# Expert blocks of a four-layer kernel: thirteen early and closed blocks in a written-out order, in place of nine

## The chip, the cores and the metric

One Trainium2 chip, one of its NeuronCores. The metric is the device time of one execution in microseconds (us), the median of several runs. Engine names as in the profile: PE is TensorE (PEld its weight loads), DVE is VectorE, ACT is ScalarE, POOL is GpSimd, SP is SyncE.

## The reference

`x` is 16 samples of 128 rows of 128 numbers, and goes through four layers, each chosen or scaled by a per-sample id:

```python
# L0: one of 8 feed-forward networks per sample, residual, layer norm with the expert's gain and shift
h = gelu(x @ Wi[e] + bi[e]);  x = layernorm(h @ Wo[e] + bo[e] + x) * gamma[e] + beta[e]
# L1: norm, film factors from a small hypernetwork, a router, two of 8 experts for every row
h = film(layernorm(x));  probs = softmax(h @ router_w);  gates, idx = top_k(probs, 2)
y = sum over the row's two experts of gates * (relu(h @ exp_w1[e] + b1[e]) @ exp_w2[e] + b2[e]);  x = x + y
# L2: a rotation of neighbouring columns by two angles per sample
# L3: a narrow adapter (128 to 32 to 32 to 128) with one of 16 expert matrices per sample, residual, layer norm
x = layernorm(up(expert_W[d] @ gelu(down(x))) + x) * gamma + beta
```

All of it is float32.

## The kernel before

**Halves and blocks.** The 16 samples are worked in four groups of four, and the expert layer in two halves of eight samples (groups 0 and 1, groups 2 and 3). Each row of 128 numbers goes to two experts, so a half has 2048 row copies. They are sorted by expert into blocks of 128 row copies, one expert per block. The full blocks of the first half can be worked before the second half has been routed: at least 9 exist, and these 9 are the early blocks (`EARLY`). What the first half leaves over is filled up with rows of the second half: together at most 39 blocks (`NBLK`), 9 early and 30 late.

**One block** passes through five engines. POOL gathers its 128 rows from `h_rows` in memory with an indirect DMA (`gather`, L536). PE transposes them (`rows_T`, L975), ACT copies the transpose out of PSUM (`transposed`, L716). PE multiplies by the block's expert matrix of 512 columns (`blk_up`, L808), which SP has loaded (`load_w1`, L440), ACT adds the bias and applies relu in four pieces (`hidden`, L726), PE multiplies back to 128 columns (`blk_down`, L808). DVE adds the expert's second bias and writes `y_blk` (`add_b2`, L1475), and POOL scatters the 128 rows to `token_rows` in memory (`scatter`, L542).

**What sets the order.** There is no scheduler: each engine runs its own program, a loop over step `k`, and semaphores hold the engines together. In step `k` PE does `blk_up(k)`, `blk_down(k-2)` and the transpose of block `k+3`; ACT does `hidden(k)` and then `transposed(k+3)`; DVE adds the bias of block `k-1`. Into the steps of the early blocks the routing of the second half is put: `z_transposes` (L877), `row_stats`, `film_h` (L631), `route`, `top2` (L1269 to L1280), `rank`, the sorting of rows into slots (`sort_slots`, `hot_blocks`, `hot_slots` L1374, `hot_tiles`, `hot_rows` L694) and `inverse`, a product on PE that turns slots into row numbers. It ends in `sources` (L1416 to L1421), which writes the row numbers `src_i` of the late blocks. `store_rows` (L639) writes the second half's `h_rows`.

**POOL's order.** The gathers of early blocks, with small powers between them for the norms (L522), then four scatters (`HELD`), then, once the late row numbers are there, four gathers, and from there one scatter and one gather in turn, the gather nine blocks ahead (`LEAD`).

**The end.** From step 30 on (`BEGIN3`) the adapter layer L3 runs for the first half in four units of two samples, two steps per unit, beside the last late blocks: `combine` on DVE (L1484, L1492) joins the two gated expert rows that SP has loaded back (`load_y`), PE does `l3_T`, `l3_down`, `l3_residual`, `l3_up`, DVE takes the statistics (`stats3`) and the inverse root by three Newton steps (`root3`). When the last block has been scattered, SP loads the second half's rows and units 4 to 7 follow.

## Time and profile before

| what | us |
|---|---|
| median of 3 runs (lowest, highest) | 231.68 (230.59, 233.28) |
| the profiled execution, its own time | 230.44 |
| its span, first to last instruction | 228.6 |
| time around the span | 1.84 |
| PE busy, share of the span | 178.3, 78% |
| DVE, ACT, POOL busy | 116.6, 107.2, 109.0 |
| mean granted TensorE clock | 0.842 of 2.4 GHz |

Times in the rows further down count from the span's start. Where a row ends in square brackets, it gives the time for which the engine sat idle just before, and after the arrow what ended it; "issue" means nothing that the profile shows. PE and PEld rows of a matrix product count two instructions for one float32 product. The granted clock is given as a share of full speed, so that 0.50 stands for 1.2 GHz and 1.00 for 2.4 GHz.

### The profile page before, as it was taken

The numbers are of one execution on the slowest core, as the hardware profiler recorded it, in microseconds if no ns is written. First come the engines' busy times: TensorE is split into PE (matmuls) and PEld (weight loads), VectorE is DVE, ScalarE is ACT, GpSimd is POOL, SyncE is SP. The second block draws the span as 40 slices with busy tenths as digits, with TensorE's granted clock in tenths as the row PEclk, the third lists the DMA queues.
The fourth block names the chain that finished last, engine by engine and source line by source line (L and its number), as shares of the span: only waits on it lengthen the run. The fifth ranks groups of instructions, "written<-read, shape, count | busy, mean of one in ns | idle before, by whom it ended". The sixth has DMA issues, their size and how long they took to land.

```text
span 228.6 us, 5312 instructions
## 1 busy us (share of the span) xinstructions
PE 178.3 (78%) x1287; PEld 161.6 (71%) x1287; DVE 116.6 (51%) x575; ACT 107.2 (47%) x338; POOL 109.0 (48%) x126
## 2 busy tenths in 40 slices
PE   6999997999959599284799888887799994077920
PEld 6999986898859599173798777876688873045710
DVE  6316798888943868940023343311236777353460
ACT  3564874665235566301566556564356651123310
POOL 5126335102870670127777777777776333101560
PEclk9999999997667859857589999999999999555555
DMA  6999999994643113047456565535951011330001
GB/s 205 294 322 337 329 317 301 250 292 123 220 130 100 26 34 106 1 104 231 137 154 186 156 173 146 147 97 173 319 167 57 26 46 47 106 134 1 26 25 44
DMA packets 35048, 34.82 MB, mean 152 GB/s; under 512 B 3793, under 2 KB 26475, under 8 KB 35019
## 3 DMA queue, kind: packets, MB, share of 16 engines
q1 hardware_dynamic: 27995, 26.56, 40.3%
q0 software_dynamic: 2496, 5.12, 7.5%
q10 hardware_dynamic: 4528, 2.81, 4.0%
q8 instruction: 12, 0.20, 0.4%
q14 instruction: 17, 0.14, 0.2%
HBM read 29.81 MB, written 4.65 MB: 151 GB/s over the span
## 4 chain that ended last, share of the span: by engine, by line
PE 35%; DVE 21%; POOL 19%; issue 11%; DMA 9%; DVEq 2%; ACT 1%; ACTq 0%; POOLq 0%; SPq 0%
PE bank L808 31%; POOL got L536 7%; POOL token_rows L542 7%; DMA got<-h_rows,src_i 6%; DVE st L1196 3%; PE bank L975 1%; POOL rstd L522 1%; DVE hot_in L1374 1%; POOL rs L556 1%; DVEq L1598 1%; DMA token_rows<-y_blk,dst_i 1%; DMA w_place<-token_rows 1%; DVE y_blk L1475 1%; DVE top_i L1272 1%; PE bank L1004 1%
## 5 line engine op out<-in xcount | busy, mean ns | idle before, releaser
L726 ACT ACTIVATE hid<-bank,small 128x128 f32<-128x128 f32 x156 | 44.4, 368 | 28.0 <-PE bank L808 27.2
L808 PE MATMUL bank<-w,hid 128*128 x312 | 46.5, 297 | 5.3 <-DVE y_blk L1475 4.8
L542 POOL DMA_INDIRECT token_rows<-y_blk,dst_i x39 | 38.8, 995 | 23.0 <-DVE y_blk L1475 13.4
L536 POOL DMA_INDIRECT got<-h_rows,src_i x39 | 38.2, 981 | 22.2 <-issue 10.1
L808 PE MATMUL bank<-gotT,w_now 128*128 128x128 f32 x312 | 46.8, 299 | 0.0
L808 PEld LDWEIGHTS bank<-w,hid 128*128 128x128 f32 x312 | 42.1, 209 | 6.3 <-issue 6.0
L808 PEld LDWEIGHTS bank<-gotT,w_now 128*128 128x128 f32 x312 | 42.9, 213 | 0.0
L1475 DVE TENSOR_TENSOR y_blk<-bank,b_tab 128x128 f32<-128x128 f32 x39 | 11.4, 291 | 58.5 <-PE bank L808 57.0
L975 PE MATMUL bank<-ident,got 128*128 128x128 f32 x39 | 13.0, 334 | 18.0 <-DMA got<-h_rows,src_i 13.2
L716 ACT ACTIVATE gotT<-bank 128x128 f32<-128x128 f32 x39 | 11.0, 282 | 27.2 <-PE bank L975 26.9
L667 ACT ACTIVATE act<-bank,small 128x128 f32<-128x128 f32 x64 | 18.0, 374 | 11.9 <-PE bank L808 11.5
L522 POOL TENSOR_TENSOR rstd<-veps,minus_half 128x4 f32<-128x4 f32 x12 | 12.3, 1027 | 20.9 <-DVE veps L1244 9.1
L975 PEld LDWEIGHTS bank<-ident,got 128*128 128x128 f32 x39 | 6.2, 160 | 22.4 <-DMA got<-h_rows,src_i 16.9
L808 PE MATMUL bank<-w_place,act 128*128 128x128 f32 x128 | 17.5, 279 | 0.7 <-ACT act L667 0.7
L808 PE MATMUL bank<-xT,w_place 128*128 128x128 f32 x128 | 17.1, 276 | 0.0
L808 PEld LDWEIGHTS bank<-w_place,act 128*128 128x128 f32 x128 | 15.5, 192 | 1.0 <-ACT act L667 0.9
L808 PEld LDWEIGHTS bank<-xT,w_place 128*128 128x128 f32 x128 | 15.6, 192 | 0.1
L1004 PE MATMUL bank<-ident,xbT 128*128 128x128 f32 x16 | 4.5, 372 | 10.7 <-DVE xbT L1492 10.7
L556 POOL TENSOR_TENSOR rs<-ve,minus_half 128x2 f32<-128x2 f32 x4 | 2.9, 714 | 18.6 <-DVE ve L1505 18.6
L1004 PEld LDWEIGHTS bank<-ident,xbT 128*128 128x128 f32 x16 | 2.3, 167 | 11.9 <-DVE xbT L1492 11.2
L749 ACT ACTIVATE zg<-bank,nmr,rs 128x128 f32<-128x128 f32 x14 | 5.6, 453 | 9.8 <-DVE nmr L1530 9.8
L808 PE MATMUL bank<-ident 128*128 128x128 f32 x38 | 8.4, 399 | 1.9 <-POOL minus_half L496 1.9
(232 smaller groups left out, 267.8 us busy)
## 6 DMA issues: line engine op xcount, KB each, us to landing
w_now<-in_exp_w SPq DMA_DIRECT2D x39, 256.0 KB, 3.3
w_place<-in_l_wi SPq DMA_DIRECT2D x16, 256.0 KB, 5.2
w_place<-in_l_wo SPq DMA_DIRECT2D x16, 256.0 KB, 5.6
rows<-in_l_rows SPq DMA_DIRECT2D x16, 128.0 KB, 4.9
w<-in_exp_w SPq DMA_DIRECT2D x8, 256.0 KB, 5.8
w_place<-token_rows SPq DMA_DIRECT2D x8, 256.0 KB, 3.5
x_sb<-in_x ACTq DMA_DIRECT2D x4, 256.0 KB, 4.5
h_rows<-h_row ACTq DMA_DIRECT2D x4, 256.0 KB, 2.8
```

The costliest lines, as they stand in the source:

```text
L522: g_.tensor_tensor(rstd[:, kind, g % 2, :], veps[:, kind, g % 2, :], minus_half[:], ALU.pow)\
L536: g_.indirect_dma_start(got[:, n % RING, :], None, h_dram[0:(HB if n < EARLY else NB) * P], bass.IndirectOffsetOnAxis(ap=src_i[:, n:n + 1] ...
L542: g_.indirect_dma_start(y_dram, bass.IndirectOffsetOnAxis(ap=dst_i[:, n:n + 1], axis=0), y_blk[:, n % YRING, :], None).then_inc(st_y[n % Y ...
L667: last = a_.activation(act0[:, b % 2, c, :], up_bank(b)[:, c * P:(c + 1) * P], ACT.Gelu, bias=cols[:, bass.ds(e * FC + (R_BI + c), 1)])
L716: a_.activation(gotT[:, n % TRING, :], got_bank, ACT.Copy).then_inc(a_gT, 1)
L726: last = a_.activation(hid[:, n % HRING, c, :], up_bank(n)[:, c * P:(c + 1) * P], ACT.Relu, bias=cols[:, bass.ds(e * FC + (R_B1 + c), 1)])
L749: last = a_.activation(z3[:, i, :], o3_bank[u][:, k * P:(k + 1) * P], ACT.Identity, bias=nmr3[:, i:i + 1], scale=rs3[:, i:i + 1])
L808: return t_.matmul(out_, lhsT, rhs, start=start, stop=stop)
L975: t_.transpose(got_bank, got[:, n % RING, :], ident[:]).then_inc(p_gT, 1)
L1004: last = t_.transpose(uT_bank[u][:, k * P:(k + 1) * P], u_b[:, place(u) + k, :], ident[:])
L1196: do(v_.bn_stats(st[:, kind, g % 2, k, :], src(k)))
L1475: v_.tensor_tensor(y_blk[:, n % YRING, :], y_bank(n), b2_tab[:, bass.ds(e, 1), :].rearrange("p o d -> p (o d)"), ALU.add)\
```

## The change

**More early blocks.** Besides the 9 blocks that are sure to be full, up to 4 blocks of the first half that are not full are closed: no row of the second half is put into them. So 13 blocks are early. Closing costs blocks: at most 41 are needed in place of 39, 13 early and 28 late.

**Order written out.** On PE and ACT the early blocks are no longer in the loop; their order stands as a list. PE does the transpose of block `k` right before `blk_up(k)`, not three blocks ahead, and ACT does `transposed(k)`, `hidden(k)` and then the copy of block `k-2`. The eight warming products ahead of the first block are gone, the two expert preparations `experts3(2)` and `experts3(3)` stand behind the last early block, and `inverse(2)` behind the transpose of block 12.

**The second bias.** For early blocks ACT copies the product out of PSUM (`evac_y`) and POOL adds the bias just before it scatters; for late blocks DVE goes on adding it. ACT also does the norm of groups 2 and 3 (`norm1`), which was DVE's. DVE's program has the whole routing of the second half in one piece.

**The end.** L3 of the first half begins at step 36 of 41 in place of 30 of 39, so that its last unit and most of its norms run behind the last block. Their inverse roots and shifts go to POOL, but for the first unit. PE reads L3's expert numbers ahead (`l3_which`).

**Small things.** `hot_slots` is two wide comparisons in place of sixteen narrow ones. `store_rows` stands earlier. The second half's last unit but one is normalised on DVE in place of ACT and POOL.

```diff
-    NBLK = (TOPK * NB * S + E1 * (P - 1)) // P
-    EARLY = -((E1 * (P - 1) - TOPK * HB * S) // P)
+    SURE = -((E1 * (P - 1) - TOPK * HB * S) // P)
+    CLOSED = 4
+    EARLY = SURE + CLOSED
...
-    RING, YRING, TRING, WRING, HRING = 16, 12, 4, 6, 3
+    RING, YRING, TRING, WRING, HRING = 16, 10, 4, 6, 3
     LEAD = 9
-    HELD = 4
+    HELD = 5
+    FIRST_OUT = 4
-    BEGIN3 = 30
+    BEGIN3 = 36
...
             def scatter(n):
-                pool.wait_ge(v_y, n + 1)
+                if n < EARLY:
+                    pool.wait_ge(a_y, n + 1)
+                    e = pool.value_load(exp_i[0:1, n:n + 1], min_val=0, max_val=E1 - 1)
+                    ch.do(g_.tensor_tensor(y_blk[:, n % YRING, :], y_blk[:, n % YRING, :],
+                                           b2_tab[:, bass.ds(e, 1), :].rearrange("p o d -> p (o d)"), ALU.add))
+                    ch.settle()
+                else:
+                    pool.wait_ge(v_y, n - EARLY + 1)
...
+                if n >= 9:
+                    scatter(n - 9)
-            hot_tiles(1)
-            for n in range(HELD):
-                scatter(n)
             hot_tiles(2)
+            for n in range(FIRST_OUT, HELD):
+                scatter(n)
...
+            for k in range(EARLY):
+                transposed(k)
+                if k == 2:
+                    norm1(2)
+                if k == 3:
+                    norm1(3)
+                if k == 5:
+                    film_h(2)
+                    film_h(3)
+                hidden(k, block_expert(k))
+                if k >= BEHIND:
+                    evac_y(k - BEHIND)
+                if k == 6:
+                    store_rows(2)
+                if k == 7:
+                    store_rows(3)
+                    hot_rows(1)
+                if k == 11:
+                    hot_rows(2)
...
-            keep_warm(8, bank[6], ident[:])
...
+            rows_T(7)
+            rank(1)
+            rows_back(2)
+            blk_up(7)
+            down_of(5)
+            rows_T(8)
+            rows_back(3)
+            blk_up(8)
+            down_of(6)
...
+            rows_T(12)
+            inverse(2)
+            blk_up(12)
+            down_of(10)
+            down_of(11)
+            down_of(12)
+            experts3(2)
+            experts3(3)
+            pe.wait_ge(v_exp, 2)
...
-                for j in range(first, past):
-                    last = v_.tensor_scalar(hot_in[:, h, j, :], col_bf[:], in_blk[:, j:j + 1], None, ALU.is_equal)
+                v_.tensor_tensor(hot_in[:, h, first:past, :],
+                                 col_bf[:].rearrange("p (o n) -> p o n", o=1).to_broadcast([P, n, P]),
+                                 in_blk_bf[:, first:past].rearrange("p (j o) -> p j o", o=1).to_broadcast([P, n, P]),
+                                 ALU.is_equal).then_inc(v_hot, 1)
...
-                if 2 <= u < HU + 2 and odd == 0:
-                    stats3(u - 2)
-                    shift_of_norm3(u - 2)
+                if u == 2 and odd == 0:
+                    stats3(0)
+                    root3(0)
+                    shift_of_norm3(0)
```

**ACT, one early block.** `gotT` is the transposed block, `hid` the hidden rows that the relu writes, `y_blk` the block's result. Before, the copy of a transpose stands between the hidden rows of two blocks and belongs to a block three further on:

```order
L719 TENSOR_LOAD exp_i
L719 ISA x2
L716 ACTIVATE gotT<-bank 128x128
L726 ISA
L726 ACTIVATE hid<-bank,small 128x128
L726 ISA
L726 ACTIVATE hid<-bank,small 128x128
```

With the change the block's own transpose comes first, then its hidden rows, then the copy of an older result, and only then the next block's transpose:

```order
L744 ACTIVATE gotT<-bank 128x128
L747 TENSOR_LOAD exp_i
L747 ISA x2
L754 ISA
L754 ACTIVATE hid<-bank,small 128x128
L754 ISA
L754 ACTIVATE hid<-bank,small 128x128
L754 ISA
L754 ACTIVATE hid<-bank,small 128x128
L754 ISA
L754 ACTIVATE hid<-bank,small 128x128
L795 ACTIVATE y_blk<-bank 128x128
```

What moved is the transpose of the next block, from two blocks ahead of its use to right behind the hidden rows of the block before.

**PE, before the second half's last routing product.** `gotT,w_now` is `blk_up`, `ident,got` a block's transpose, `hot_blk,hot_in` the product `inverse`. Before, the first part of `inverse` for the late blocks stands right ahead of block 8's `blk_up`, whose transpose was done steps earlier:

```order
L808 MATMUL bank<-w,hid 128x128
L808 MATMUL bank<-hot_blk,hot_in 128x60 x16
L808 MATMUL bank<-gotT,w_now 128x128 x4
L1042 TENSOR_LOAD exp_i
L1042 ISA x2
L808 ISA
L808 MATMUL bank<-w,hid 128x128
```

With the change each `blk_up` has its own transpose right ahead of it, here that of block 10 with the first part of `inverse` between:

```order
L1034 MATMUL bank<-ident,got 128x128
L865 MATMUL bank<-hot_blk,hot_in 128x56 x16
L865 MATMUL bank<-gotT,w_now 128x128 x4
L1102 TENSOR_LOAD exp_i
L1102 ISA x2
L865 ISA
L865 MATMUL bank<-w,hid 128x128
```

What moved is the transpose, which now waits for a gather and is waited for within one step; the second part of `inverse` stands in the same way behind the transpose of block 12.

**POOL, where the late row numbers arrive.** `got` is a gathered block, `token_rows` the memory that results are scattered to. Before, four gathers and then one scatter and one gather in turn:

```order
L528 TENSOR_TENSOR hot_blk<-hot_tmp,col_bf 128x16x30
L536 DMA got<-h_rows,src_i 128x128 x4
L542 DMA token_rows<-y_blk,dst_i 12288x128
L536 DMA got<-h_rows,src_i 128x128
L542 DMA token_rows<-y_blk,dst_i 12288x128
L536 DMA got<-h_rows,src_i 128x128
```

With the change one gather, and then a scatter that has the addition of the bias ahead of it:

```order
L548 DMA got<-h_rows,src_i 128x128
L555 TENSOR_LOAD exp_i
L555 ISA x2
L556 ISA
L556 TENSOR_TENSOR y_blk<-y_blk,b_tab 128x128
L561 DMA token_rows<-y_blk,dst_i 12288x128
L548 DMA got<-h_rows,src_i 128x128
L555 TENSOR_LOAD exp_i
L555 ISA x2
L556 ISA
```

Eight such scatters (blocks 5 to 12) are left at that point, where five plain ones (blocks 4 to 8) were, and each has one late gather behind it.

## Rows read from the trace of the kernel before

**Rows 1.** Chain of work that ended last: start us, us, what.

```profile
86.38 0.29 DVE top_v L1269 x4
...
101.35 1.00 POOL got L536
...
102.66 3.49 DMA got<-h_rows,src_i
```

**Rows 2.** Timeline, from the early row numbers to the sorting: start us, us, engine, instruction.

```profile
54.57 0.17 DVE L1421 TENSOR_SCALAR src_i<-dst_i 128x9 int32<-128x9 int32 x1
...
84.83 0.39 DVE L1269 MAX8 top_v<-bank 128x8 f32<-128x8 f32 x4 [0.37 <-issue]
...
88.63 0.60 ACT L639 ACTIVATE h_row<-bank 128x512 f32<-128x512 f32 x1 [0.38 <-PE bank L894]
...
89.25 0.37 ACTq L641 DMA_DIRECT2D h_rows<-h_row  x1
...
90.21 0.62 PE L808 MATMUL bank<-hot_blk,hot_in 128*128 128x60 bf16 x16
...
93.58 3.48 DVE L1374 TENSOR_SCALAR hot_in<-col_bf,in_blk 128x128 bf16<-128x128 bf16 x16
```

**Rows 3.** Timeline, one step of a block at full and at half clock.

```profile
61.43 0.28 ACT L716 ACTIVATE gotT<-bank 128x128 f32<-128x128 f32 x1 [2.82 <-PE bank L975]
...
61.82 0.14 PEld L975 LDWEIGHTS bank<-ident,got 128*128 128x128 f32 x1 [0.73 <-issue]
...
111.95 1.83 PEld L808 LDWEIGHTS bank<-gotT,w_now 128*128 128x128 f32 x8
...
114.23 1.14 ACT L726 ACTIVATE hid<-bank,small 128x128 f32<-128x128 f32 x4 [0.61 <-PE bank L808]
...
119.40 0.97 PEld L808 LDWEIGHTS bank<-gotT,w_now 128*128 128x128 f32 x8
...
120.72 1.14 ACT L726 ACTIVATE hid<-bank,small 128x128 f32<-128x128 f32 x4 [0.37 <-PE bank L808]
...
121.73 0.29 ACT L716 ACTIVATE gotT<-bank 128x128 f32<-128x128 f32 x1
```

**Rows 4.** Windows: stretch, length, busy us (x instructions) of PE, PEld, DVE, ACT, POOL, clock, DMA, GB/s.

```profile
54.00:58.00 4.00, 4.00 (x24) 3.06 (x21) 3.73 (x21) 1.31 (x3) 2.04 (x2) 0.52 0.46 135
...
72.00:78.00 6.00, 4.07 (x37) 3.87 (x35) 4.85 (x30) 1.82 (x7) 3.35 (x4) 1.00 0.05 12
78.00:82.00 4.00, 3.64 (x17) 3.64 (x18) 3.42 (x12) 4.00 (x14) 2.76 (x3) 0.51 0.07 18
...
135.00:150.00 15.00, 12.42 (x97) 11.03 (x96) 5.22 (x11) 9.63 (x32) 11.64 (x12) 1.00 0.54 146
...
191.00:200.00 9.00, 0.07 (x1) 0.00 (x0) 4.63 (x22) 0.81 (x2) 1.84 (x2) 0.67 0.32 97
200.00:210.00 10.00, 7.80 (x28) 5.26 (x28) 5.29 (x22) 2.52 (x7) 0.75 (x1) 0.50 0.22 78
```

**Rows 5.** Groups by line, shapes apart: busy us, mean ns of one, idle before.

```profile
L631 ACT ACTIVATE hT<-bank,film 128x128 f32<-128x128 f32 x16 | 6.1, 495 | 6.4 <-DVE film L1262 6.4
...
L548 POOL TENSOR_TENSOR zg<-zg,rows 128x256 f32<-128x256 f32 x3 | 2.2, 726 | 0.0
...
L694 ACT ACTIVATE hot_blk<-hot_tmp,pair_no 128x240 bf16<-128x240 bf16 x4 | 1.8, 529 | 0.6 <-DVE hot_tmp L1367 0.6
...
L1367 DVE TENSOR_TENSOR hot_tmp<-col_bf,blk_of_bf 128x480 bf16<-128x480 bf16 x2 | 1.3, 657 | 0.4 <-issue 0.4
```

**Rows 6.** Timeline, the last gather and transpose, the last addition, the second half's first unit.

```profile
172.53 0.97 POOL L536 DMA_INDIRECT got<-h_rows,src_i  x1 [0.30 <-PE bank L975]
...
178.21 0.27 PE L975 MATMUL bank<-ident,got 128*128 128x128 f32 x1
...
194.51 0.29 DVE L1475 TENSOR_TENSOR y_blk<-bank,b_tab 128x128 f32<-128x128 f32 x1
...
200.51 0.61 DVE L1484 SCALAR_TENSOR_TENSOR z<-w_place,gates,x 128x128 f32<-128x128 f32 x2 [4.13 <-DMA w_place<-token_rows]
```

More of the change, by code:

```diff
@@ L46, in conditional_layers_kernel, with most_blocks @@
     KT = TOPK * HB
-    NBLK = (TOPK * NB * S + E1 * (P - 1)) // P
-    EARLY = -((E1 * (P - 1) - TOPK * HB * S) // P)
+    SURE = -((E1 * (P - 1) - TOPK * HB * S) // P)
+    CLOSED = 4
+    EARLY = SURE + CLOSED
+    def most_blocks(full):
+        closed = max(EARLY - full, 0)
+        held = min((E1 - closed) * (P - 1), TOPK * HB * S - full * P)
+        return full + closed + (TOPK * HB * S + held + E1 * (P - 1)) // P
+    NBLK = max(most_blocks(full) for full in range(SURE, TOPK * HB * S // P + 1))
     LATE = NBLK - EARLY
@@ L474, in _ @@
                         load_y(u)
-            for u in range(HU):
-                store_out(u)
+            store_out(0)
             scattered(NBLK)
@@ L479, in _ @@
                 load_y(u)
-            for u in range(HU, NU):
+            for u in range(1, NU):
                 store_out(u)
@@ L687, in _ @@
                     film_h(1)
-                if b == 14:
-                    store_rows(0)
+                if b >= 13 and b < 13 + HG:
+                    store_rows(b - 13)
             def hot_rows(s):
@@ L705, in _ @@
             a_.activation(warm[:, 2, :], ones_row[:], ACT.Exp).then_inc(ac, 1)
-            for i in range(NG):
-                evac_m3(i)
+            evac_m3(0)
+            evac_m3(1)
             for i in range(E3, MT):
@@ L744, in norm3 @@
                 act.wait_ge(v_nmr3, u + 1)
-                if earlier(u) is not None:
-                    act.wait_ge(v_o3, earlier(u) + 1)
+                if earlier(u) == 0:
+                    act.wait_ge(v_o3, 1)
+                elif earlier(u) is not None:
+                    act.wait_ge(g_o3, earlier(u))
                 for k in unit(u):
@@ L1590, in _ @@
             l0_spread_shift(3)
+            minus_mean(2)
             l1_stats(3)
-            l1_norm(2)
-            l1_norm(3)
+            hot_blocks(1)
+            minus_mean(3)
+            later_bases()
+            row_stats(2)
+            row_stats(3)
+            film_factors(2)
+            film_factors(3)
+            part_experts()
+            top2(2)
+            top2(3)
+            ranks(1)
+            more_blocks()
+            sort_slots(1)
+            hot_blocks(2)
+            hot_slots(1, 0, KT // 2)
@@ L1652, in _ @@
+            combine(HU - 1, unit(HU - 1))
+            scale_shift3(0)
+            stats3(1)
+            stats3(2)
+            shift_of_norm3(1)
+            shift_of_norm3(2)
             combine(HU, unit(HU))
+            stats3(3)
             combine(HU + 1, unit(HU + 1))
+            shift_of_norm3(3)
             combine(HU + 2, unit(HU + 2))
```

321 lines of the change are left out of this document (178 added, 143 removed).

## The prediction

> **What bounds the kernel now.** I read the chain of waits first. It shows three stages behind the first layer. Until 101.35 the chain goes through DVE's ranking and sorting of the second half, top values from 86.38 on [rows 1]. Then POOL issues the first late gather, and the next 1.31 us later (102.66 [rows 1]); from there one issue follows another. The last of the 30 late gathers is issued at 172.53 [rows 6]. Between the two lie 29 gathers and 26 scatters, 55 issues in 71.2 us, 1.294 us each: a block costs POOL 2.59 us, and POOL paces this stage. PE is busy 12.42 of 15 us in it at full clock [rows 4]. Third comes the end. The last transpose runs at 178.21, the last addition of the bias at 194.51, and the second half's first unit starts 6.0 us later, when its rows are back [rows 6]. From the last addition to the end of the execution there are 230.44 - 194.51 = 35.9 us.
>
> So the time is a sum of three: when the late row numbers arrive, how long POOL needs to the last gather, and how long it takes from there to the last addition. I go through the change by these.
>
> **Part 1: the early blocks, up to the late row numbers.** Block 0 can be gathered once its row numbers exist, at 54.74 before [rows 2]. The change widens the comparisons: DVE took 3.48 us for sixteen when the second half was sorted [rows 2]; the nearest row for a wide one is 657 ns for 480 elements [rows 5], in proportion 1.40 us for 1024, 2.8 us for two. Against that stand four small instructions more for the closed blocks, 0.17 us each by the row of `src_i` [rows 2]. I take no difference, with 1 us either way as bound. Gather 0 is issued at about 55.1 and lands 3.5 us later, as the first late one did, 3.49 [rows 1]: 58.6. PE stood at half clock from 54 on, 0.52 [rows 4], and the warming products are gone, so the first steps run at half.
>
> The Trainium skill, "VectorE: DVE Perf Modes", section on the perf-mode tier table, says that a two-tensor operation on 16-bit data runs at two elements per cycle. The row above, 16-bit throughout, is at 1.37 ns an element and does not show it; by the rule the row numbers would come about 1 us earlier and the total would be 1 us less.
>
> Now one step. ACT's program runs transposed copy, hidden rows, copy of an older result, next transposed copy, and PE's `blk_up` waits for the transposed copy: a ring. At full clock: from `blk_up` to the hidden rows 119.40 to 120.72, 1.32 us; to ACT's next start 121.73, 1.01; the copy of the older result about 0.26, a quarter of the four hidden pieces; from transposed copy to PE's next start 61.43 to 61.82, 0.39 [rows 3]. Together 3.0 us. At half clock the first link is 111.95 to 114.23, 2.28 [rows 3], and the ring 3.7 without and 3.94 with the older copy, 4.6 where that copy waits for PE's `blk_down`, which at half comes 1.8 us later (the weight loads of 1.83 [rows 3]).
>
> Starts of `blk_up` so: block 0 at 59.5 (landing, transpose, copy). Blocks 1 and 2 at 63.2 and 66.9, half clock. Block 3 at 71.5 (4.6), block 4 at 75.8 (4.3), by when I take the clock to have risen, since PE is then busy without a gap. Block 5 at 78.8 (3.0). In step 5 two `film_h` stand in the ring, 6.1 / 4 = 1.5 us each [rows 5], of which 1.3 is covered by `blk_up`: 1.6 more, block 6 at 83.4. In step 6 ACT's `store_rows(2)` waits for PE's `rows_back(2)`, that for `rank`, that for `top2(3)` on DVE, that for `route(3)`, which stands behind `blk_up(6)`. `blk_up` takes 0.97 [rows 3], `route` has as many products, from the start of `top2(3)` to `store_rows` it was 86.38 to 88.63, 2.25 us, and `store_rows` takes 0.60 and its DMA's issue 0.37 [rows 1, 2]; with the transposed copy that is 5.7: block 7 at 89.1. Step 7 holds `store_rows(3)`, 1.0 us, and `hot_rows(1)`, two of 0.529 that overlap a little (1.8 / 2 = 0.9 a pair [rows 5]): block 8 at 94.0. Three steps of 3.0 bring block 11 to 103.0. Behind its hidden rows ACT copies block 9 and does `hot_rows(2)`, until 106.5. Only then can PE do `inverse(2)`, 0.62, and DVE the row numbers, three instructions of 0.17 with a wait ahead of each, some 0.7 [rows 2]. DVE's own sorting is long done by then, since its program no longer waits for blocks. First late gather at 108.1 in place of 101.35: **+6.7 us**.
>
> Bounds: at full clock from the start, 4.2 us less (0.7, 0.7, 1.6, 1.2 in the first four steps); at half clock to the end, 8 steps x 1.5 = 12 us more.
>
> **Part 2: POOL to the last gather.** The late gathers are 13 to 40, and between first and last stand 27 more gathers and 27 scatters: 54 x 1.294 = 69.9 us. Closing has made two blocks more, which is why this is hardly less than the 71.2 before. Eight scatters carry an addition. No such instruction is in the trace of before; the nearest is POOL's 128x256 at 726 ns [rows 5], so 128x128 lies between 0.36 and 0.73; I take 0.55. The expert number is read ahead of it: DVE idled 0.37 us where it read one [rows 2]. POOL's queue could hide that (0) or take 0.6. I take 0.9, between 0.35 and 1.3: 8 x 0.9 = 7.2, from 2.8 to 10.4. Behind a scatter so delayed the next gather is queued, and PE waits for that one, so nothing covers it. Sum 77.1 in place of 71.2: **+5.9 us**. Last gather at 185.2.
>
> **Part 3: from the last gather to the last addition.** Before, 172.53 to 194.51, 22.0 us: PE was late (last transpose 178.21, not 176.0, where the gather landed), and PE had nothing left from 191.1 on (0.07 us busy in the window from 191 [rows 4]) while DVE did statistics and Newton steps ahead of the last addition, 3.4 us. With the change PE has only begun with L3 when the last gather lands, 3.5 us after its issue; and only unit 0's statistics stand in DVE's loop, three blocks ahead of the end. From the last transpose to PE's end it was 191.1 - 178.2 = 12.9 us; the same products and half a unit more of L3, less waiting, 13.2. So 3.5 + 13.2 = 16.7: **-5.3 us**.
>
> **Part 4: behind the last addition.** DVE now does there what it did before: `combine(3)`, `scale_shift3(0)`, statistics of units 1 and 2. It was idle 4.13 us before the second half's rows came [rows 6] and was busy 4.63 in the window from 191 [rows 4], so the work about fits. Behind it one more unit's statistics stand between two combines; the numbers read ahead and the last unit but one on DVE save about as much. I take **0**, from -3.9 (half of the 7.8 us for which PE is busy at clock 0.50 from 200 to 210 [rows 4], if its new work keeps the clock up) to +2.
>
> **Sum.** 6.7 + 5.9 - 5.3 + 0 = +7.3 on the profiled execution's own 230.44 is 237.7. That execution was 0.5% under the median of the runs shown, 231.68; I say 238. About 1% is what a measurement of this kernel can tell from no change.
>
> **The clock.** Early blocks leave PE idle about a third of each step. For a clock that holds: 12.42 of 15 us busy holds 1.00, and 72 to 78 held it with 4.07 of 6. Against: 78 to 82 is at 0.51 behind it, and 200 to 210 stays at 0.50 although PE is busy 7.80 of 10 us [rows 4]. The Trainium skill, "TensorE: Matmul & The Clock Gate", section on what is actually happening, calls the slow clock the default that activity releases. The last window shows busy time that released nothing; by the rule alone part 1 stands, by that window its upper bound does.
>
> **Rivals.**
> *No change (0.17).* The clock is full from block 0 (-4.2) and POOL reads expert numbers while it still issues (2.8 in place of 7.2, -4.4): 237.7 - 8.6 = 229.1, within 1% of 230.44. For it: 72 to 78. Against: PE is idle ahead of block 0.
> *Faster (0.16).* The ring doesn't bind: steps come at the pace of the busiest engine, 2.0 us for PE, as the late blocks come at about 1.9 when nothing is awaited (hidden rows at 120.72, `blk_up` 119.40 [rows 3]). Then the DVE sorting sets the row numbers, at some 97, 11 us sooner: 226.6. For it: neither PE nor ACT has more than 2 us of work in a step. Against: the order rows, in which the next transposed copy stands behind the hidden rows. It decides from a mean of 3.2 us per step from block 0 to 12 (mine is 3.85); below that the change gains.
> *Much slower (0.10).* PE stays at half clock through the early blocks: +12, 249.7.
> The forecast itself has 0.57.
>
> **How the numbers follow.** Faster by over 1%: 0.16, the ring rival. Within 1%: 0.17. Slower by over 1%: 0.57 + 0.10 = 0.67. The likeliest case alone runs from 233 to 243, additions and single clock drops; the range reaches to the no-change case and to about the middle of the way to the half-clock case: 228.5 to 246.
>
> **What would show it.** The first late gather between 106 and 111; hidden rows of neighbouring early blocks 3.0 us apart at full clock; POOL's additions 0.4 to 0.7 us and pairs of about 3.5 us for eight blocks; the last gather to the last addition about 17 us. Wrong if the first late gather comes by 101, if early steps stand 2 us apart, or if the eight pairs come at 2.6.

## The result and the profile after

The changed kernel takes 239.01 us (median of 4 runs, 236.76 to 239.58) against 231.13 of the kernel before on the same chip: ratio 1.040, 95% interval 1.034 to 1.046. The forecast was 238.0. The profiled execution took 238.47, its span is 236.7, the mean granted clock 0.829 in place of 0.842. By the prediction's four parts, each from the rows below and [rows 1, 6]:

| part | before | after | change | forecast |
|---|---|---|---|---|
| start to the first late gather | 101.35 | 111.41 | +10.1 | +6.7 |
| first to last late gather | 71.2 | 73.3 | +2.1 | +5.9 |
| last gather to last addition | 22.0 | 18.4 | -3.6 | -5.3 |
| last addition to the execution's end | 35.9 | 35.4 | -0.6 | 0 |
| sum | 230.44 | 238.47 | +8.0 | +7.3 |

The chain of waits of the changed kernel, part of the early stage (start us, us, what). It answers to [rows 1]:

```profile
87.61 0.92 PE bank L954 x4
88.56 0.61 ACT h_row L668
89.19 0.37 ACTq L670
89.65 0.29 ACT gotT L744
89.98 3.78 PE bank L865 x16
...
103.60 1.17 PE bank L865 x8
105.21 0.51 ACT hid L754 x2
...
106.45 2.05 PE bank L865 x16
```

Before, the chain went through DVE's sorting here. Now it alternates between PE and ACT: that is the ring. At 87.61 it shows something more, the rows' way back on PE, the storing of rows on ACT and its DMA issue, one behind the other, before the next transposed copy.

The timeline of the changed kernel, one plain step at full clock and then the starts of `blk_up` of blocks 6 to 8 (start us, us, engine, instruction, idle before). It answers to [rows 3]:

```profile
75.87 0.97 PEld L865 LDWEIGHTS bank<-gotT,w_now 128*128 128x128 f32 x8 [0.48 <-ACT gotT L744]
77.19 1.14 ACT L754 ACTIVATE hid<-bank,small 128x128 f32<-128x128 f32 x4 [1.36 <-PE bank L865]
78.20 0.29 ACT L795 ACTIVATE y_blk<-bank 128x128 f32<-128x128 f32 x1
78.36 0.30 ACT L744 ACTIVATE gotT<-bank 128x128 f32<-128x128 f32 x1
78.72 0.97 PEld L865 LDWEIGHTS bank<-gotT,w_now 128*128 128x128 f32 x8 [0.92 <-ACT gotT L744]
82.88 0.97 PEld L865 LDWEIGHTS bank<-gotT,w_now 128*128 128x128 f32 x8 [1.30 <-ACT gotT L744]
89.98 1.78 PEld L865 LDWEIGHTS bank<-gotT,w_now 128*128 128x128 f32 x8 [1.86 <-ACT gotT L744]
96.80 0.97 PEld L865 LDWEIGHTS bank<-gotT,w_now 128*128 128x128 f32 x8 [2.39 <-ACT gotT L744]
```

PE waits for ACT's transposed copy ahead of each of these. The plain step takes 2.85 us (75.87 to 78.72): 1.32 to the hidden rows, 1.01 and 0.16 to the next transposed copy, 0.36 back to PE. The two steps behind block 6 take 7.10 and 6.82.

The windows of the changed kernel (stretch, length, busy us and instructions of PE, PEld, DVE, ACT, POOL, clock, DMA share, GB/s). They answer to [rows 4]:

```profile
59.00:66.00 7.00, 4.51 (x18) 3.85 (x19) 5.22 (x28) 1.59 (x6) 5.86 (x6) 0.50 0.66 206
...
78.00:82.00 4.00, 2.99 (x26) 2.86 (x25) 3.65 (x13) 4.00 (x15) 3.31 (x5) 1.00 0.57 148
82.00:90.00 8.00, 5.66 (x32) 5.19 (x32) 5.25 (x41) 3.13 (x11) 6.50 (x9) 0.63 0.32 85
90.00:100.00 10.00, 7.86 (x38) 7.26 (x38) 7.21 (x18) 4.30 (x14) 7.11 (x7) 0.67 0.33 94
100.00:111.00 11.00, 8.38 (x90) 7.76 (x90) 0.41 (x3) 5.54 (x22) 0.00 (x0) 0.95 0.32 107
...
185.00:203.00 18.00, 16.17 (x122) 13.80 (x120) 6.77 (x31) 8.52 (x28) 8.42 (x9) 1.00 0.11 38
...
210.00:220.00 10.00, 8.37 (x31) 5.56 (x30) 6.46 (x26) 3.05 (x8) 4.21 (x6) 0.50 0.23 71
```

The clock is at half in the first steps, full from 78 to 82, and lower again from 82 to 100. From 100 to 111 POOL does nothing and DVE almost nothing: POOL waits for the late row numbers, and DVE for the product on PE from which it computes them.

POOL's timeline in the changed kernel, where these arrive:

```profile
111.41 0.97 POOL L548 DMA_INDIRECT got<-h_rows,src_i  x1 [13.39 <-DVE src_i L1544]
112.41 0.47 POOL L556 TENSOR_TENSOR y_blk<-y_blk,b_tab 128x128 f32<-128x128 f32 x1
113.15 0.98 POOL L561 DMA_INDIRECT token_rows<-y_blk,dst_i  x1 [0.28 <-ACT y_blk L795]
114.43 0.97 POOL L548 DMA_INDIRECT got<-h_rows,src_i  x1 [0.30 <-issue]
```

POOL had been idle for 13.39 us. From gather to gather, with one scatter and its addition between, it takes 3.02.

The timeline of the changed kernel at the end, which answers to [rows 6]: last gather, last transpose and last addition:

```profile
184.71 0.98 POOL L548 DMA_INDIRECT got<-h_rows,src_i  x1 [0.30 <-issue]
...
187.22 0.33 PE L1034 MATMUL bank<-ident,got 128*128 128x128 f32 x1
...
203.12 0.29 DVE L1598 TENSOR_TENSOR y_blk<-bank,b_tab 128x128 f32<-128x128 f32 x1 [3.21 <-PE bank L865]
```

The last addition waits for PE, which is busy 16.17 of the 18 us before it. The chain of waits of the changed kernel shows for what PE itself waited there (start us, us, what):

```profile
195.57 0.41 DVE st L1623 x2
...
198.79 0.81 ACT zg L779 x2
199.65 0.71 PE bank L865 x4
200.37 1.45 issue
201.82 1.17 PE bank L865 x8
```

The groups by line, shapes apart, give the sizes of two new instructions (busy us, mean ns of one, idle before), beside [rows 5]:

```profile
L556 POOL TENSOR_TENSOR y_blk<-y_blk,b_tab 128x128 f32<-128x128 f32 x13 | 7.0, 540 | 0.3
...
L1489 DVE TENSOR_TENSOR hot_in<-col_bf,in_blk_bf 128x1024 bf16<-128x1024 bf16 x4 | 5.8, 1487 | 0.0
```

### The profile page after: what moved, and what is told of

The parts are those of the page before. It is cut to its first block, busy times and chain, and to the rows that moved or that the text cites. A ratio compares the mean times of both kernels' runs of the same rounds, so it can differ in the third digit from the quotient of the medians.

```text
span 236.7 us, 5387 instructions
## 1 busy us (share of the span) xinstructions
PE 186.8 (79%) x1305; PEld 167.0 (71%) x1305; DVE 107.2 (45%) x499; ACT 114.5 (48%) x367; POOL 127.0 (54%) x150
## 4 chain that ended last, share of the span: by engine, by line
PE 36%; POOL 14%; DMA 13%; issue 13%; DVE 11%; ACT 5%; ACTq 2%; POOLq 1%; DVEq 0%
PE bank L865 32%; DMA got<-h_rows,src_i 9%; POOL got L548 6%; POOL token_rows L561 5%; DMA small<-in_small 2%; ACT hid L754 2%; PE bank L1034 2%; DMA w_place<-token_rows 1%; DVE hot_in L1489 1%; DVE st L1303 1%; DVE xbT L1615 1%; ACT gotT L744 1%; DMA token_rows<-y_blk,dst_i 1%; POOL y_blk L556 1%; ACT hT L660 1%
## 5 line engine op out<-in xcount | busy, mean ns | idle before, releaser
L754 ACT ACTIVATE hid<-bank,small 128x128 f32<-128x128 f32 x164 | 46.9, 370 | 42.0 <-PE bank L865 42.0
L865 PE MATMUL bank<-gotT,w_now 128*128 128x128 f32 x328 | 53.4, 315 | 10.1 <-ACT gotT L744 8.8
L865 PEld LDWEIGHTS bank<-gotT,w_now 128*128 128x128 f32 x328 | 47.9, 224 | 13.2 <-ACT gotT L744 11.5
L865 PE MATMUL bank<-w,hid 128*128 x328 | 50.1, 301 | 1.7 <-issue 1.6
L865 PEld LDWEIGHTS bank<-w,hid 128*128 128x128 f32 x328 | 45.1, 213 | 3.0 <-issue 2.6
L1598 DVE TENSOR_TENSOR y_blk<-bank,b_tab 128x128 f32<-128x128 f32 x28 | 8.2, 292 | 64.3 <-PE bank L865 62.8
L1034 PE MATMUL bank<-ident,got 128*128 128x128 f32 x41 | 14.0, 341 | 18.4 <-DMA got<-h_rows,src_i 17.6
L534 POOL TENSOR_TENSOR rstd<-veps,minus_half 128x4 f32<-128x4 f32 x12 | 12.7, 1058 | 22.1 <-DVE veps L1354 10.1
L1303 DVE BATCH_NORM_STATS2 st<-bank 128x6 f32<-128x128 f32 x32 | 7.1, 283 | 9.5 <-PE bank L937 6.3
L865 PE MATMUL bank<-x_sb,xT 128*128 128x128 f32 x32 | 8.2, 401 | 1.6 <-ACT zg L779 1.6
L865 PEld LDWEIGHTS bank<-x_sb,xT 128*128 128x128 f32 x32 | 6.2, 273 | 4.2 <-ACT zg L779 2.3
L528 POOL TENSOR_TENSOR xbT<-xT,bo_cols 128x512 f32<-128x512 f32 x4 | 4.3, 1066 | 8.8 <-ACT xT L652 4.6
```

Of the source, the lines that this page charges most:

```text
L528: g_.tensor_tensor(xbT[:, g % 2].rearrange("p (b s) -> p b s", b=GS), xT[:, g % 2].rearrange("p (b s) -> p b s", b=GS), over_tokens(bo_col ...
L534: g_.tensor_tensor(rstd[:, kind, g % 2, :], veps[:, kind, g % 2, :], minus_half[:], ALU.pow)\
L754: last = a_.activation(hid[:, n % HRING, c, :], up_bank(n)[:, c * P:(c + 1) * P], ACT.Relu, bias=cols[:, bass.ds(e * FC + (R_B1 + c), 1)])
L865: return t_.matmul(out_, lhsT, rhs, start=start, stop=stop)
L1034: t_.transpose(got_bank, got[:, n % RING, :], ident[:]).then_inc(p_gT, 1)
L1303: do(v_.bn_stats(st[:, kind, g % 2, k, :], src(k)))
```

## The experiments

The theory after reading the two traces: the late row numbers come 10 us later because the product that gives them stands at the end of thirteen early steps, and these are long because each block's transpose, its copy, its products and its hidden rows stand one behind the other on PE and ACT. The rivals: the clock; the routing of the second half; POOL's additions; the two blocks more; or that PE would be no sooner whatever comes earlier. Each kernel starts from the changed one, 239.01 us. The kernel before ran beside each group of them and took 229.4 to 231.0 us there, where it took 231.13 beside the changed one; so of a difference to 239.01 up to 1.8 us can lie in this, and the ratio to the kernel before (1.040 for the changed one) is given as well. Block 0 is transposed between 58.8 and 61.7 in the executions read, so first late gathers of two kernels compare to some 2 us; steps from block to block compare better.

**The ring undone.** PE transposes block k+1 ahead of the products of block k, ACT copies it ahead of the hidden rows of block k.

```diff
+            transposed(0)
             for k in range(EARLY):
-                transposed(k)
+                if k + 1 < EARLY:
+                    transposed(k + 1)
...
             rows_T(0)
-            blk_up(0)
             rows_T(1)
+            blk_up(0)
+            rows_T(2)
             blk_up(1)
...
```

> The changed kernel with one thing undone in the written-out order: PE transposes block k+1 ahead of the products of block k, and ACT copies that transpose ahead of the hidden rows of block k. Theory (the early blocks are slow because transposed copy, products, hidden rows and next transposed copy form a ring of 2.85 us per step): neighbouring hidden rows come 2.0 to 2.5 us apart where nothing else is awaited, PE idles less so that its clock falls less, the first late gather comes at 101 to 106 in place of 111.4, and the total is 5 to 10 us below the changed kernel, 229 to 234. Rival (the early stage is set by the clock and by what the routing of the second half waits for, not by the ring): steps stay at 2.8 us or more, first late gather 110 or later, total within 2 us of 239.

Measured: 226.4 us, 12.6 less, more than the theory asked; 0.980 of the kernel before (0.971 to 0.989). The timeline of this kernel, six starts of `blk_up` (blocks 0 to 2 and 9 to 11) and the first late gather:

```profile
62.79 1.91 PE L867 MATMUL bank<-gotT,w_now 128*128 128x128 f32 x8
...
65.25 1.91 PE L867 MATMUL bank<-gotT,w_now 128*128 128x128 f32 x8
...
67.17 1.86 PE L867 MATMUL bank<-gotT,w_now 128*128 128x128 f32 x8
...
90.88 1.12 PE L867 MATMUL bank<-gotT,w_now 128*128 128x128 f32 x8
...
93.35 1.14 PE L867 MATMUL bank<-gotT,w_now 128*128 128x128 f32 x8
...
95.33 1.06 PE L867 MATMUL bank<-gotT,w_now 128*128 128x128 f32 x8
...
100.19 0.97 POOL L548 DMA_INDIRECT got<-h_rows,src_i  x1 [4.33 <-DVE src_i L1546]
```

Blocks 9 to 11, at full clock, give steps of 2.47 (a part of the product for the row numbers is in it) and 1.98, where a plain step of the changed kernel takes 2.85; at half clock, which both kernels have in their first steps (0.50 from 60 to 66 in the changed one, from 62 to 68 in this), 2.46 and 1.92 in place of 3.59. So the ring shows at either level of the clock. The first late gather comes at 100.19. Hidden rows of blocks 0 and 12 stand 35.5 us apart (64.86 to 100.39), 2.96 a step, where the changed kernel's `blk_up` needs 4.14 (60.63 to 110.29). The ring is the main cost, and without it the rest of the change is a gain. The 12.6 us are not the plain steps alone. `blk_up` of blocks 0 and 12 stands 36.3 us apart here (62.79 to 99.09) in place of 49.7, 13.4 less; 6.5 of these lie in the two steps behind block 6 (7.5 in place of 13.9), in which the routing no longer stands in a ring and the clock is higher (0.79 from 82 to 90 and 1.00 from 90 to 100, where the changed kernel has 0.63 and 0.67).

**The late row numbers' product two steps sooner.**

```diff
-                if k == 11:
+                if k == 8:
                     hot_rows(2)
...
             inverse(1)
+            inverse(2)
             blk_up(10)
...
-            inverse(2)
             blk_up(12)
```

> The changed kernel with the last part of the product that gives the late row numbers right behind its first part, two steps sooner (at block 10 in place of block 12), and the rows it needs from ACT at step 8 in place of 11. DVE's own sorting was done at 97.6 and waited 12.9 us. Theory (the late row numbers come late only because this product stands at the end of the early steps): first late gather at 104.5 to 106.5 in place of 111.4, total 4 to 6 us lower, 233 to 235. Rival (the early blocks themselves must be finished anyway, PE or POOL catches up no sooner): the gather comes sooner but the last addition moves by less than 2 us, total 237 or more.

Measured: first late gather at 103.45, total 233.03, 6.0 less; 1.011 of the kernel before (1.001 to 1.020). The rival falls: what comes sooner there ends sooner. The gather came 8.0 us sooner, a little more than expected; the clock was higher here too, 0.92 in place of 0.63 from 82 to 90.

**Nine scatters ahead of the first late gather** (`HELD` = 9 in place of 5).

> The changed kernel with nine scatters in place of five ahead of the first late gather (blocks 5 to 8 too), in the 13.4 us in which POOL waits for the late row numbers. Theory (POOL paces the late stage, 1.29 us an issue and 0.46 us an addition): between the first and the last late gather stand 4 scatters and 4 additions fewer, 4 x 1.75 = 7.0 us; the first late gather stays at 111.4, the last comes at 177 to 179 in place of 184.7, total 4 to 7 us lower, 232 to 235. Rival (PE is nearly as late, it is busy 21.6 of the 25 us from 160 to 185): POOL's gain turns into waits for PE, total within 2 us of 239.

Measured: 230.65 us, 8.4 less and more than expected, 1.003 of the kernel before (0.998 to 1.007). From first to last late gather it takes 66.5 us (113.89 to 180.35) in place of 73.3, so 6.8 of the 7.0 expected. The execution read took 235.54 us, well above the median, and all its gathers come late; but the kernel further down with nine scatters first and the transposes ahead needs 66.3 for the same stretch. POOL does pace the late stage, and the 13.39 us for which it stood idle were worth filling.

**The additions left out.** POOL scatters the early blocks without their second bias.

```diff
                 if n < EARLY:
                     pool.wait_ge(a_y, n + 1)
-                    e = pool.value_load(exp_i[0:1, n:n + 1], min_val=0, max_val=E1 - 1)
-                    ch.do(g_.tensor_tensor(y_blk[:, n % YRING, :], y_blk[:, n % YRING, :],
...
-                    ch.settle()
```

> The changed kernel without POOL's addition of the second bias for the early blocks (their second bias is left out of the result) and without the reading of the expert number ahead of it. Theory (an addition costs POOL 0.46 us and eight of them stand between late gathers): pairs of scatter and gather take 2.56 us from the first one, last gather 3.5 to 4 us sooner, total 3 to 4 us lower, 235 to 236. Rival (the additions are hidden, by PE or by the queue): less than 1 us.

Measured: 234.25 us, 4.8 less, 1.015 of the kernel before (1.007 to 1.022). First late gather at 111.57, last at 181.28, 69.7 us between, 3.6 less; 54 issues at 1.294 are 69.9. The rest of the 4.8 lies within the spread of both kernels' runs (236.8 to 239.6, 233.3 to 235.3).

**PE kept busy in its waits.** Products without use in the bank that the block's own products fill next.

```diff
+            def warm_up(n, count):
+                if n >= 2:
+                    pe.wait_ge(a_hid, n - 1)
+                keep_warm(count, up_bank(n), ident[:])
+
+            warm_up(0, 8)
...
             rows_T(0)
+            warm_up(0, 2)
             blk_up(0)
...
             rows_T(7)
+            warm_up(7, 6)
             rank(1)
...
```

> The changed kernel with PE kept busy in its waits of the early stage: eight products without use ahead of block 0 and two (six in steps 7 and 8) between each block's transpose and its own products. The ring of 2.85 us per step at full clock stays. If the clock's falls (0.50 from 59 to 72, and again behind 85) are a large part of what the early stage takes, the granted clock stays near 1.00 from 60 to 111, plain steps stay at 2.85 to 3.3 us, the first late gather comes at 102 to 106 in place of 111.4 and the total is 4 to 8 us lower, 231 to 235. If the clock falls all the same or the products without use stand in the ring's way, first late gather at 109 or later and total 237 or more.

Measured: 237.66 us, 1.4 less; first late gather at 110.18. This is the second case of the expectation. The gain itself isn't clear of noise: 1.030 of the kernel before (1.023 to 1.036), against 1.040 (1.034 to 1.046). The windows of this kernel:

```profile
66.00:72.00 6.00, 5.00 (x43) 4.67 (x42) 2.07 (x11) 5.14 (x18) 2.36 (x2) 1.00 0.60 185
...
82.00:90.00 8.00, 6.54 (x46) 6.29 (x45) 4.43 (x31) 2.30 (x7) 6.22 (x8) 0.79 0.38 102
90.00:100.00 10.00, 7.84 (x54) 7.42 (x53) 6.56 (x14) 4.58 (x15) 6.42 (x6) 0.83 0.31 88
```

The clock is full from 66 to 82, and blocks 0 to 6 take 19.1 us (62.05 to 81.18) in place of 22.25 (60.63 to 82.88). But the two steps behind block 6 stay at 8.0 and 6.4 us. The products ahead of the ranking and of the rows' way back take 1.9 and 1.5 us of them; without these it would be some 11.0 for both, against 13.9 in the changed kernel. So the clock is worth 3.1 us in the first steps (22.25 - 19.13) and, as an estimate, 2.9 in these two, but is not all that makes them long. The estimate takes the useless products to lie wholly in the ring, and the clock was not full in these windows (0.79 and 0.83). One of the two steps can be read without it: with the late row numbers' product two steps sooner, the order up to there the same and the clock full until 88, the step behind block 6 took 6.01 us (82.57 to 88.58) in place of 7.10, so that 1.1 us of that step were the clock's.

**No block closed**: 9 early and 30 late, the written-out order cut after block 8.

```diff
-    CLOSED = 4
+    CLOSED = 0
...
-    FIRST_OUT = 4
+    FIRST_OUT = 0
...
-    BEGIN3 = 36
+    BEGIN3 = 34
...
-                if k == 11:
+                if k == 8:
                     hot_rows(2)
...
             rows_back(3)
+            inverse(1)
             blk_up(8)
             down_of(6)
-            rows_T(9)
-            blk_up(9)
+            inverse(2)
             down_of(7)
...
             down_of(8)
...
```

> The changed kernel with no block closed: 9 early and 30 late blocks, 39 in all, its written-out order cut after block 8 (transposes still right ahead of their own block), both parts of the product for the late row numbers beside block 8, four scatters more behind the early gathers, L3 begun five steps before the end as in the changed kernel. If the closed blocks cost time because four more steps of the ring stand ahead of the late row numbers, first late gather at 98 to 101, 54 issues and 4 additions to the last gather (54 x 1.294 + 4 x 0.46 = 71.7), 18.4 and 35.3 behind it as in the changed kernel, total 223 to 227. If the written-out order costs the time whatever the number of early blocks, total 235 or more.

Measured: 230.09 us, 0.995 of the kernel before (0.990 to 1.000): between the two. First late gather at 104.58, behind both the row numbers at 102.5 and a fifth scatter at 103.30; 71.3 us to the last, as expected (71.7). The row numbers are later than I expected because blocks 7 and 8 go at half clock here too and ACT's rows for the product come at 100.45. So with the ring kept, four steps and two blocks fewer take 8.9 us off: 6.8 up to the first late gather and 2.0 from there to the last. With the ring undone thirteen blocks (226.4) beat nine with it; nine without it were not run, so what closing is worth by itself stays open.

**The routing moved aside, the ring kept.** PE does the products of blocks 7 and 8 first; ACT stores rows while it would wait for products.

```diff
             rows_T(7)
+            blk_up(7)
             rank(1)
             rows_back(2)
-            blk_up(7)
...
+            blk_up(8)
             rows_back(3)
-            blk_up(8)
...
+                if k == 8:
+                    store_rows(2)
+                if k == 9:
+                    store_rows(3)
+                    hot_rows(1)
                 hidden(k, block_expert(k))
...
-                if k == 6:
-                    store_rows(2)
-                if k == 7:
-                    store_rows(3)
-                    hot_rows(1)
```

> The changed kernel with the ring kept (each transpose right ahead of its own block) but the second half's routing moved out of it: PE does the products of blocks 7 and 8 ahead of the ranking and of the rows' way back, and ACT stores rows and prepares the one-hot rows of the second sorting stage while it would wait for the products of blocks 8 and 9 anyway, not ahead of the next transposed copy. In the changed kernel these two steps took 7.1 and 6.8 us (starts 82.88, 89.98, 96.80). If they were long because routing stood in the ring, they come to 3 to 4.5 us each, the first late gather at 104 to 107 in place of 111.4 and the total 4 to 7 us lower, 232 to 235. If they were long because the clock stood at half or because DVE was late, steps 6 to 8 stay above 6 us and the total within 2 us of 239.

Measured: 232.41 us, 6.6 less, 1.007 of the kernel before (1.004 to 1.011); first late gather at 103.64. The timeline and the windows of this kernel:

```profile
82.95 0.97 PEld L865 LDWEIGHTS bank<-gotT,w_now 128*128 128x128 f32 x8 [1.22 <-ACT gotT L744]
86.44 0.97 PEld L865 LDWEIGHTS bank<-gotT,w_now 128*128 128x128 f32 x8 [0.66 <-ACT gotT L744]
89.55 0.97 PEld L865 LDWEIGHTS bank<-gotT,w_now 128*128 128x128 f32 x8 [0.66 <-ACT gotT L744]
```

```profile
78.00:90.00 12.00, 9.39 (x79) 8.64 (x78) 9.17 (x52) 8.57 (x31) 9.80 (x13) 1.00 0.35 106
```

The steps behind block 6 take 3.49 and 3.11 us in place of 7.10 and 6.82. But the clock stays full too, and its fall in the changed kernel lies at 84, where the order of the two is still the same. So a half of the edit was run as well, ACT's part alone.

```diff
+                if k == 8:
+                    store_rows(2)
+                if k == 9:
+                    store_rows(3)
+                    hot_rows(1)
                 hidden(k, block_expert(k))
...
-                if k == 6:
-                    store_rows(2)
-                if k == 7:
-                    store_rows(3)
-                    hot_rows(1)
```

> Half of the edit that moved the routing aside: ACT stores rows and prepares the one-hot rows in the waits of steps 8 and 9, but PE still does the ranking and the rows' way back ahead of the products of blocks 7 and 8. The whole edit gave 232.41 us, steps of 3.5 and 3.1 us behind block 6, and a clock that did not fall at 85, although the order is the same as in the changed kernel up to there. If the fall of the clock at 85 belongs to the order up to block 7, it is here too (0.6 to 0.8 from 82 to 90), the two steps take 4.5 to 6 us each and the total is 234 to 237. If it doesn't fall here either, the steps take 3.5 to 5 us and the total is 232.5 to 235; then the changed kernel's fall hangs on more than the order.

Measured: 233.0 us, 6.0 less; first late gather at 105.67. Beside it the kernel before took 229.4, so the ratio, 1.019 (1.010 to 1.028), says less: about 4.7 us under the changed kernel's 1.040. Its windows:

```profile
82.00:90.00 8.00, 6.00 (x53) 5.67 (x53) 6.14 (x42) 3.93 (x17) 6.61 (x9) 1.00 0.40 110
90.00:100.00 10.00, 7.55 (x74) 6.76 (x72) 7.98 (x19) 6.43 (x25) 7.62 (x8) 1.00 0.29 85
```

The clock doesn't fall here either, and the two steps take 4.29 and 3.71 us (83.84, 88.13, 91.84). Read beside each other, both at full clock: PE's part of the edit is worth 1.4 us in these steps (8.0 against 6.6). ACT's is some 3 (11.0, the estimate above, against 8.0) and the clock's some 2.9 of the changed kernel's 13.9; these two hang on that estimate. What decides the fall stays open: of seven kernels read for this, with the same order on PE and ACT up to there, it came at 83 to 86 in four (the changed one, the one without additions, the one with nine early blocks, the one with nine scatters first), at 88 in the one with the row numbers sooner, and not at all in these two.

**Together.** First the ring undone and nine scatters first:

> The transposes one block ahead on PE and ACT (which alone gave 226.4 us) together with nine scatters ahead of the first late gather (which alone gave 230.65). If POOL still paces the late stage, the gains add: 6 to 8 us under 226.4, 218.5 to 220.5, with the first late gather at 100 and the last at 166 to 168. If PE has become the bound of the late stage (in the first of the two it was busy 19.7 of the 20 us from 160 to 180), the gain is less than 2 us, 225 or more. I expect something between, 221 to 224, because PE was idle 12 of the 49 us from 111 to 160 and earlier gathers fill that.

Measured: 222.06 us, 0.959 (0.953 to 0.965) of the kernel before; between the two, as expected. The timeline of POOL in it, around the first late gather:

```profile
101.65 0.98 POOL L561 DMA_INDIRECT token_rows<-y_blk,dst_i  x1 [0.28 <-POOL y_blk L556]
102.94 0.97 POOL L548 DMA_INDIRECT got<-h_rows,src_i  x1 [0.30 <-issue]
```

The gather no longer waits for row numbers, computed from 98.45 on, but for the scatters ahead of it. That is why the next kernel, with `inverse(2)` ahead of block 11 and `hot_rows(2)` at step 9 besides, gained nothing:

> As the run before it in this group, and the last part of the product for the late row numbers one step sooner (ahead of block 11's products in place of block 12's, ACT's rows for it after step 9 in place of 11). DVE's sorting was done at 94.9 with the transposes ahead, and its next instruction waited 4.4 us. If the row numbers still set the start of the late stage, first late gather at 97 to 99 and 1 to 3 us less than the run without this; if PE bounds the late stage, no difference.

Measured: 222.47 us, 0.964 of the kernel before (0.958 to 0.970). I had named PE as the reason for no difference; it was POOL, whose first late gather came at 100.57, 0.30 behind a scatter, although the computing of the row numbers began at 92.85. That it lies 2.4 us ahead of the 102.94 above is not the edit's doing: block 0 was transposed 2.6 us sooner in this execution (58.81 against 61.36). Then the second bias of blocks 9 to 12 by DVE (a constant `BY_ACT` = 9 in place of `EARLY` where ACT copies and POOL adds):

> Transposes ahead and nine scatters first (222.06 us), and the second bias of early blocks 9 to 12 added by DVE as for late blocks, in place of ACT's copy and POOL's addition. Four additions of 0.47 us leave POOL's path between first and last late gather: if POOL paces, 1.5 to 2 us less, 220 to 220.6; if PE does, no difference.

Measured: 221.53 us, 0.962 of the kernel before (0.955 to 0.968); 0.5 less is within the runs' spread (220.2 to 224.0), so the total doesn't tell. The traces do for POOL: from first to last late gather it is 64.5 us in place of 66.3, 1.8 of the 1.9 expected. Last, all of it, with `HELD` = 7:

> Everything that gained, together: transposes ahead, routing beside the steps, late row numbers' product ahead of block 11, seven scatters ahead of the first late gather, second bias of blocks 9 to 12 by DVE. Row numbers at about 94 (DVE's sorting done at 92 to 95), first late gather 95 to 97, then 52 issues x 1.294 + 2 x 0.47 = 68.2 to the last, 18.4 and 35.3 behind it: 217 to 220. If PE bounds the late stage whatever comes earlier, 221 or more, as with the run that had the row numbers sooner and gained nothing (222.47 against 222.06).

Measured: 220.98 us, 0.963 (0.956 to 0.971) of the kernel before. The waits of POOL from 90 to 170 in it (what waited, on what, us in total, times, longest):

```profile
POOL got L549 <- issue: 7.9, 26, 0.3
POOL token_rows L562 <- issue: 7.0, 23, 0.3
POOL token_rows L562 <- POOL y_blk L557: 1.7, 6, 0.3
POOL got L549 <- PE bank L1035: 0.6, 2, 0.3
POOL token_rows L562 <- DVE y_blk L1599: 0.6, 2, 0.3
```

POOL has no wait over 0.3 us left from 90 to the last gather. The total is 1 us above the range I gave: the row numbers were computed from 94.28 on, as expected, but POOL was not through with its seven scatters and came to the first late gather at 99.05, not at 95 to 97. From there to the last it took 67.6 (forecast 68.2) and behind it 18.4 and 35.2. The last four kernels, 220.98 to 222.47, can't be told apart; all beat both the kernel before and the changed one.

## Why the prediction was right, and where its sizes were off

**Part 1, the mechanism.** Right: the ring binds, the first late gather comes when the last early steps are done, and DVE's sorting is ready long before (its last instruction ahead of the wait at 97.42, the next at 110.52). The ring's terms were 3.0 us at full clock and 3.7 at half; measured 2.85 and 3.59 (60.63 to 64.22). Block 0 came at 60.63 (forecast 59.5), block 5 at 78.72 (78.8), block 6 at 82.88 (83.4). Undoing the ring gave back more than the whole loss.

**Part 1, the size.** The failed step is "by when I take the clock to have risen", which I then let stand for all that follows: block 7 at 89.1, block 8 at 94.0. Measured 89.98 and 96.80, 13.9 us for two steps in place of 10.6, 3.3 too little and as much as the whole miss. At full clock the same two steps come to about 11 by the estimate above, near the working's 10.6; the clock had fallen again, to 0.63 and 0.67. That block 6 was met so well (82.88 for 83.4) is partly luck: block 0 came 1.1 us late, and the six steps behind it took 22.25 us in place of 23.9. Behind block 8 the forecast ran about parallel: 9.65 us to block 11 (106.45) for 9.0, and from the start of `inverse(2)` to the first late gather 1.5 us (109.91 to 111.41), for which the working had 1.6.

**Part 2.** +2.1 in place of +5.9. The count of issues was right (54 without additions measured 69.7, working 69.9). The mis-sized term is the addition with the reading of its expert number: 0.9 taken, 0.46 measured (pairs of 3.03 against 2.56). The addition alone is 0.47 (112.41), near the 0.55 taken for it, so the reading costs POOL nothing on top; the rest of the 0.9, and the 0.6 allowed for the reading, stood on no row of POOL. The bound's lower end, 0.35, was the nearer.

**Part 3.** -3.6 in place of -5.3. The gather was transposed 2.5 us behind its issue, not 3.5, but PE then needed 15.9 us to the last addition, not 13.2. The chain shows where: unit 0's statistics and Newton steps on DVE (195.57 to 198.77) lie on it, the bit that I had put "three blocks ahead of the end", then ACT's normalising, PE's residual product, and 1.45 us in which PE waits for nothing that the profile shows ahead of the last `blk_down`. This was read, not tried.

**Part 4.** -0.6, forecast 0. PE's new work at the end didn't bring the clock up: 0.50 from 210 on, as before.

**Two rules weighed.** The wide comparisons took 1487 ns for 1024 elements, 1.45 ns each, much as the row of before had it (1.37). The Trainium skill's rate of two elements per cycle for 16-bit data ("VectorE: DVE Perf Modes", section on the perf-mode tier table) doesn't show here. One operand of these comparisons is a single number per slot, spread over 128 columns (`to_broadcast` in the diff), so they are no test of the rate for two plain tensors. With products in PE's waits the clock was at 1.00 from 66 to 72, where the changed kernel had 0.50. That agrees with the Trainium skill, "TensorE: Matmul & The Clock Gate", section on what is actually happening, by which activity releases the slow clock. The end of the kernel doesn't show it: there PE was busy 8.37 of 10 us and stayed at 0.50.

**The rivals.** "The ring doesn't bind" was to decide at 3.2 us a step; the mean was 4.14, so it was out for the changed kernel, and it describes the kernel with the ring undone (2.96 a step, 226.4; its price was 226.6). The row that it names for 1.9 us a step doesn't show that by itself, but the trace of before does (`blk_up` at 117.51, 119.40 and 121.30), and with the ring undone a step at full clock came down to 1.98. The rival with no change asked for a full clock from block 0, which the trace doesn't have; its other half, expert numbers read while POOL still issues, held (3.7 us for eight additions, 2.8 in its price). The half-clock rival was half true: blocks 0 to 3, which the forecast had, and 6 to 8, which it had not.

The errors had opposite signs, 3.3 us too little in part 1 and 1.7 in part 3, 3.8 too much in part 2 and 0.6 in part 4; the nearness of the sum owes something to that.

## What to carry to other kernels

When an order is written out by hand for engines that run in order, write down for each step who waits for whom: if the next block's first instruction stands behind this block's last on one engine, the step is as long as the whole way round, however idle the engines are. Fetch and transpose one block ahead, and put other work where the engine would wait, not between two links of the ring. Then look at what the engine that paces the next stage does while it waits, since work due later can be done there for nothing.

## What the runs showed that I had not expected

- A copy of 0.29 us on ACT delays the next one by 0.16 only (78.20 to 78.36, and likewise 103.09 to 103.25 and 105.93 to 106.09): these neighbours on ACT overlap, and the ring is shorter than the sum of its durations.
- The clock fell a second time in the middle of the early stage, and not in every kernel with the same order up to there (1.00 from 82 to 90 in one, 0.63 in another). It can't be read from the order alone.
- Undoing one ring gave 12.6 us, moved scatters 8.4 and moved routing 6.6. They don't add up: all together, with two smaller edits, gave 18.0. Ring and routing meet in the same two steps behind block 6 (6.5 and 7.3 us less there), and the scatters fill the wait of POOL that the other two shorten.
